# Expert weights applied to summed second products, with ScalarE's squares and roundings and the router's steps in another order

## What is computed

```python
# attention layer, feed-forward
u, g = split(y @ w_swiglu.T); x = x + u * silu(g) @ w_out.T
# experts, on z = layernorm(x)
probs = softmax(z @ w_router.T); top = argmax(probs); weight = probs[top]
h = z @ w_fc[e].T                          # e = 0, 1
a = square(where(h >= 0, h, 0.5 * h))
x = x + sum over e of (top == e) * weight * (a @ w_proj[e].T)
```

## Time and profile before

| | us |
|---|---|
| median of 3 runs | 862.57 (862.54 to 862.64) |
| the profiled execution | 862.95 |
| its span, first to last instruction | 860.8 |
| busy: TensorE, VectorE, ScalarE, GpSimd | 851.4, 683.3, 554.7, 370.6 |
| granted TensorE clock | 1.00 over the span |

### The profile page before, as it was taken

How to read it: one execution, slowest core, us unless ns; L and a number is a source line. 1 busy time by engine, 2 the same in 40 slices (tenths; PEclk the granted TensorE clock), 3 DMA queues, 4 the chain that set the end, 5 groups by cost and what they waited for, 6 DMA issues and landing times.

```text
span 860.8 us, 14422 instructions
## 1 busy us (share of the span) xinstructions
PE 851.4 (99%) x4618; PEld 731.0 (85%) x4618; DVE 683.3 (79%) x1075; ACT 554.7 (64%) x1009; POOL 370.6 (43%) x215
## 2 busy tenths in 40 slices
PE   8999999999999999999999999999999999999998
PEld 7888888888888888888888888888888889878767
DVE  5777777777777777777777777888888878779897
ACT  5666666666666666666666666666777656676563
POOL 2555454544555554445445555544454433220000
DMA  7212214010101010010101010101101000679740
GB/s 271 98 51 76 73 52 167 24 49 24 49 24 49 24 49 25 30 43 24 49 24 49 24 49 24 48 25 28 46 24 49 26 1 11 239 282 410 308 147 13
DMA packets 19529, 66.25 MB, mean 77 GB/s; under 512 B 2224, under 2 KB 2992, under 8 KB 19120
## 3 DMA queue, kind: packets, MB, share of 16 engines
q1 hardware_dynamic: 19072, 64.88, 20.9%
q10 hardware_dynamic: 432, 1.05, 0.3%
HBM read 65.66 MB, written 0.26 MB: 77 GB/s over the span
## 4 chain that ended last, share of the span: by engine, by line
PE 91%; issue 4%; DVE 2%; DMA 1%; POOL 1%; ACT 0%; POOLq 0%; ACTq 0%; SPq 0%; DVEq 0%
PE kv_ps L879 11%; PE f_ps L866 11%; PE v_bank L784 10%; PE v_bank L785 10%; PE v_bank L786 10%; PE k_bank L784 10%; PE k_bank L785 10%; PE k_bank L786 10%; PE kv_ps L1178 2%; PE kv_ps L1160 1%; DMA early<-in_wk 1%; PE f_ps L949 0%; PE f_ps L1050 0%; PE v_bank L968 0%; DMA ctx_raw<-in_ctx 0%
## 5 line engine op out<-in xcount | busy, mean ns | idle before, releaser
L461 POOL TENSOR_TENSOR ksum_acc<-ksum_acc,kf 128x1024 f32<-128x1024 f32 x97 | 233.0, 2402 | 86.7 <-DVE kf L1284 86.7
L454 POOL TENSOR_TENSOR ctx_lo<-ctx_raw,ctx_hi 128x512 fp32r<-128x512 f32 x92 | 119.7, 1301 | 274.0 <-ACT ctx_hi L532 274.0
L540 ACT ACTIVATE keys<-k_bank,bias_cols 64x512 fp32r<-64x512 f32 (+1 forms) x194 | 131.5, 678 | 148.6 <-PE k_bank L786 146.2
L1260 DVE SCALAR_TENSOR_TENSOR keys<-k_bank,bias_cols,keys 64x512 fp32r<-64x512 f32 (+1 forms) x194 | 143.2, 738 | 83.7 <-ACT keys L540 80.4
L1277 DVE TENSOR_TENSOR kf<-f_ps,fb 128x256 f32<-128x256 f32 x392 | 148.6, 420 | 16.8 <-ACT fb L557 5.6
L784 PE MATMUL v_bank<-wv_hi,ctx_lo 128*128 128x512 f32 x388 | 152.3, 392 | 0.0
L785 PE MATMUL v_bank<-wv_lo,ctx_hi 128*128 128x512 f32 x388 | 152.1, 392 | 0.0
L784 PE MATMUL k_bank<-ctx_hi,wk_lo 128*128 128x512 f32 (+1 forms) x392 | 151.4, 386 | 0.0
L785 PE MATMUL k_bank<-ctx_lo,wk_hi 128*128 128x512 f32 (+1 forms) x392 | 151.1, 385 | 0.0
L786 PE MATMUL v_bank<-wv_hi,ctx_hi 128*128 128x512 f32 x388 | 151.0, 389 | 0.0
L786 PE MATMUL k_bank<-ctx_hi,wk_hi 128*128 128x512 f32 (+1 forms) x392 | 149.9, 383 | 0.0
(11 more groups left out here) (245 smaller groups left out, 979.0 us busy)
## 6 DMA issues: line engine op xcount, KB each, us to landing
ctx_raw<-in_ctx SPq DMA_DIRECT2D x46, 512.0 KB, 3.3
early<-in_stream SPq DMA_DIRECT2D x15, 1024.0 KB, 8.4
raw<-in_stream SPq DMA_DIRECT2D x12, 1024.0 KB, 8.7
early<-in_stream SPq DMA_DIRECT2D x8, 512.0 KB, 4.2
early<-in_ctx SPq DMA_DIRECT2D x2, 512.0 KB, 6.1
early<-in_wv SPq DMA_DIRECT2D x1, 1024.0 KB, 7.8
early<-in_wq SPq DMA_DIRECT2D x1, 1024.0 KB, 9.2
early<-in_wo SPq DMA_DIRECT2D x1, 1024.0 KB, 7.1
```

Source lines behind the costliest of these rows:

```text
L454: pool.tensor_tensor(ctx_lo[:, s, :, cols], raw[:, :, t % 2 * P:(t % 2 + 1) * P], ctx_hi[:, s, :, cols].bitcast(f32), ALU.subtract).then_i ...
L461: pool.tensor_tensor(ksum_acc[:, :].rearrange("p (j f) -> p j f", f=P), ksum_acc[:, :].rearrange("p (j f) -> p j f", f=P), kf[:, t % 2, :, ...
L540: act.activation(keys_2[rows, s, 2 * m + h, 0:n], src[rows, 0:n], ACT.Identity, bias=bias_cols[rows, KC + m:KC + m + 1]).then_inc(k_hi_rea ...
L1260: dve.scalar_tensor_tensor(out=keys_2[other, s, 2 * m + h, 0:n], in0=src[rows, 0:n], scalar=bias_cols[rows, KC + m:KC + m + 1], in1=keys_2 ...
```

## The change

- The router's weight is no longer part of `hid`. `hid` is the plain square, and is made by ACT (`expert_square`, from DVE's maximum in `gate`) in place of DVE. The second products of each expert are summed apart, expert 0 in `wide_ps[0]`, expert 1 in `wide_ps[1]` and the two last halves, and DVE adds each sum times its weight to `x1`: a further `wide_added(GP[3], ...)` in block 6.
- One second product is fp32 and seven are in three passes (before: two and six). So 52 half groups are rounded, not 50.
- ACT's roundings in the experts stand elsewhere: none in block 0, GP[1] in block 1, then two groups in each of blocks 2 to 5, and one in 6 and 7. DVE's pieces are set to match.
- The router: the logits are scaled on DVE behind the maximum of block 0, the exponentials stand on ACT behind its square, and the six steps behind the pieces of block 3. A dummy exponential ahead of the experts sets ACT's table. POOL subtracts the mean that DVE subtracted at the output.
- SwiGLU: Silu on ACT in place of Sigmoid on ACT and a product on DVE; a dummy Silu ahead of it.
- Attention: denominators and numerators in another order on PE; two of ACT's roundings are split around other steps, its copy of the router weights stands behind the exponentials; DVE runs one piece ahead of the wait for `rms_ready` and two behind it (before: two, then one).

```diff
-         GF_[5], GP[3], GF_[6], GP[4], GF_[7], *GP[5:8]]
-FIRST = 2
+SPLIT = [..., *GF_[0:4], GP[1],
+         GF_[4], GP[2], GF_[5], GP[3], GF_[6], GP[4], GF_[7], *GP[5:8]]
-        wide_ps = kv_bank[0]
+        wide_ps = [kv_bank[0], kv_bank[2]]
...
             rstd(3, 8, 1)
+            pool.wait_ge(actT_done, 8)
+            pool.tensor_scalar(x1[:, :], x1[:, :], stat[:, 18:19], None, ALU.subtract).then_inc(mean_back, 1)
...
             turned_high(3)
+            act.activation(stat[:, 30:31], half[:, :], ACT.Silu)
             weight_high(GD[0])
...
-                act.activation(gate[:, n % 2, :], k_ps[n % 2], ACT.Sigmoid).then_inc(gateg_ready, 1)
+                act.activation(gate[:, n % 2, :], k_ps[n % 2], ACT.Silu).then_inc(gateg_ready, 1)
...
             turned_high(4)
+            act.activation(stat[:, 30:31], half[:, :], ACT.Exp)
             def expert_high(n):
                 act.wait_ge(group_used, GF_[n] + 1)
-                if n >= 2:
-                    act.wait_ge(hid_ready, nd + n - 1)
                 act.activation(gate[:, n % 2, :], k_ps[n % 2], ACT.Copy, scale=0.5)\
                    .then_inc(fc_half_ready, 1)
-            act.wait_ge(logit_neg_ready, 1)
-            act.activation(logit[:, 3:5], logit[:, 0:2], ACT.Exp, bias=logit[:, 2:3]).then_inc(expl_ready, 1)
+            def expert_square(n):
+                if n >= 2:
+                    act.wait_ge(hidT_done, nd + n - 1)
+                act.wait_ge(fc_ready, n + 1)
+                act.activation(hid[:, n % 2, :], gate[:, n % 2, :], ACT.Square).then_inc(hid_ready, 1)
             for n in range(2 * nd):
                 expert_high(n)
                 if n:
                     hidden_turned(nd + n - 1)
-                for g in (GF_[4:5], GP[2:3], GF_[5:6], (GP[3], GF_[6]), (GP[4], GF_[7]), GP[5:7], GP[7:8], ())[n]:
+                expert_square(n)
+                if n == 0:
+                    act.wait_ge(logit_neg_ready, 1)
+                    act.activation(logit[:, 3:5], logit[:, 0:2], ACT.Exp, bias=logit[:, 2:3]).then_inc(expl_ready, 1)
+                for g in ((), GP[1:2], (GF_[4], GP[2]), (GF_[5], GP[3]), (GF_[6], GP[4]), (GF_[7], GP[5]), GP[6:7], GP[7:8])[n]:
                     weight_high(g)
...
-            denominators(range(3))
+            denominators(range(4)).then_inc(den_done, 1)
...
-            denominators(range(3, 4)).then_inc(den_done, 1)
-            denominators(range(4, NPAIR)).then_inc(den_done, 1)
+            denominators(range(4, 6))
             numerators(0)
+            denominators(range(6, NPAIR)).then_inc(den_done, 1)
             numerators(1)
...
-            low_pieces(1, 3)
+            low_pieces(1, 2)
+            dve.wait_ge(rms_ready, 1)
+            low_pieces(2, 4)
             dve.wait_ge(wr_hi_ready, 1)
...
-            low_pieces(26, 27)
+            low_pieces(26, 28)
...
             for n in range(2 * nd):
                 dve.wait_ge(fc_half_ready, n + 1)
                 h = gate[:, n % 2, :]
-                link(dve.tensor_tensor(h, k_ps[n % 2], h, ALU.max))
-                dve.scalar_tensor_tensor(out=hid[:, n % 2, :], in0=h, scalar=logit[:, 6 + e:7 + e], in1=h,
-                                         op0=ALU.mult, op1=ALU.mult).then_inc(hid_ready, 1)
-                if n > FIRST:
+                dve.tensor_tensor(h, k_ps[n % 2], h, ALU.max).then_inc(fc_ready, 1)
+                if n == 0:
+                    router_logits()
+                if n > 1:
                     hidden_low(nd + n - 1)
-                low_pieces(*((27, 28), (28, 30), (30, 34), (34, 38), (38, 42), (42, 44), (44, 48), (48, 50))[n])
+                low_pieces(*((28, 29), (29, 32), (32, 36), (36, 40), (40, 44), (44, 48), (48, 50), (50, 52))[n])
+                if n == 3:
+                    router_weights()
+                if n == 6:
+                    dve.wait_ge(mean_back, 1)
+                    wide_added(GP[3], logit[:, 6:7])
```

More of the change, by code:

```diff
@@ L1147, in hidden_turn, with down_outs, hidden_down @@
                 transposes(f_ps[n % 2], hid[:, n % 2, :]).then_inc(hidT_done, 1)
[L1149 to L1155, removed]
+            def down_outs(g, last_one):
+                return [(half_ps[b][:, 0:D // 2], halves[b]) for b in range(2)] if last_one else [(wide_ps[g > GP[3]], full)]
+            def hidden_down(n, g):
                 wait_loaded(pe, g)
                 pe.wait_ge(hidT_ready, n + 1)
[L1158 to L1163, removed]
+                for k in range(KC):
+                    last = pe.matmul(wide_ps[0], hid_T2[n % 2][:, k, :], raw(g)[:, k, :], start=k == 0, stop=False)
                 last.then_inc(group_used, 1)
@@ L1544, in _ @@
                 dve.wait_ge(group_used, GU[n] + 1)
-                dve.tensor_tensor(hid[:, n % 2, :], v_ps[n % 2], e, ALU.mult).then_inc(hid_ready, 1)
+                dve.tensor_tensor(hid[:, n % 2, :], v_ps[n % 2], gate[:, n % 2, :], ALU.mult).then_inc(hid_ready, 1)
                 if n:
@@ L1574, in _, with router_logits @@
[L1574 to L1575 removed]
+            low_pieces(26, 28)
+            def router_logits():
+                dve.wait_ge(logit_done, 1)
+                dve.wait_ge(rstd_ready, 3)
+                dve.tensor_tensor(stat[:, 13:14], stat[:, 8:9], stat[:, 8:9], ALU.mult)
+                link(dve.tensor_scalar(logit[:, 0:2], v_ps[0][:, 0:2], stat[:, 8:9], None, ALU.mult))
+                link(dve.scalar_tensor_tensor(out=logit[:, 0:2], in0=v_ps[0][:, 2:4], scalar=stat[:, 8:9], in1=logit[:, 0:2],
+                                              op0=ALU.mult, op1=ALU.add))
+                link(dve.tensor_reduce(logit[:, 2:3], logit[:, 0:2], AX.X, ALU.max))
+                dve.tensor_scalar(logit[:, 2:3], logit[:, 2:3], -1.0, None, ALU.mult).then_inc(logit_neg_ready, 1)
@@ L1594, in _ @@
                     dve.wait_ge(group_used, GP[-1] + 1)
-                dve.scalar_tensor_tensor(out=hid[:, 0, cols], in0=half_ps[b][:, 0:D // 2], scalar=stat[:, 18:19],
-                                         in1=x1[:, cols], op0=ALU.subtract, op1=ALU.add).then_inc(out_ready, 1)
+                dve.scalar_tensor_tensor(out=hid[:, 0, cols], in0=half_ps[b][:, 0:D // 2], scalar=logit[:, 7:8],
+                                         in1=x1[:, cols], op0=ALU.mult, op1=ALU.add).then_inc(out_ready, 1)
 def kernel(**inputs):
```

75 lines of the change are left out of this document (36 added, 39 removed).

## The result

| us | before | after |
|---|---|---|
| median of 8 runs | 862.62 (862.51 to 863.05) | 865.89 (864.25 to 866.26) |
| the profiled execution, its span | 862.95, 860.8 | 866.26, 864.2 |
| granted TensorE clock, mean of the span | 1.00 | 0.998 |

The medians differ by 3.3 us, and the change makes the kernel slower. The ratio estimated over all executions is 1.0033, with an interval of 1.0024 to 1.0041 (the medians alone give 1.0038). The forecast was 864.1 us, within 0.2% of no change. The median lies 1.8 us above it and 0.3 above the upper end of the range; by the ratio (1.0033 of 862.57 is 865.4) the result is just inside the range. The case that came true is "slower by over 0.2%", which had 0.36. Six of the eight executions show a mean clock of 0.998 and take 865.82 to 866.26; the two at 1.000 take 864.25 and 864.92.

What follows compares the result with a forecast made beforehand. TensorE, with 91% of the chain of waits, was taken to bound the kernel. Experts -1.34 - 0.64 + 3.83, rounded to +1.8, and attention -0.3 gave +1.5 us on 862.57: 864.1 us, range 862.2 to 865.6.

Steps and rivals of the forecast that it cites:

- slower by over 0.2%: Outcome case for the whole kernel: measured time over 0.2% above before; takes the second, third and fourth rival, chance 0.36.
- the loop: Experts: DVE max, ACT square, first w_hi, four w_lo pieces, next max strictly in turn; 6.88 us against PE's 6.04.
- Everything from there to the end is the same work.: After the last turn of hid, turn(7) at 853.83: nothing further changes, so its +1.8 us carries to the end.
- The loop and no early gain: Rival: same loop with square and handovers at upper bounds (+0.4), or attention's 0.3 lost; 864.5 to 865, chance 0.28.
- attention's end: Denominator j=3 ahead of the transposes and an earlier GpSimd root: about 0.4 and more, of which 0.3 us reaches the end.
- The stalls: Experts: PE waits of 0.84, 0.87 and 2.12 us before turns 5, 6 and 7 of hid; turn 4 just in time.
- the two late pieces: Attention's end: two DVE pieces behind rms_ready take 2.27 us, freeing DVE for the reciprocal at 763.3, not 763.60.
- the removed stall at 762.29: Attention's end: PE's stall of 0.45 us should go, but PE's wait at 768.53 grows.
- The removed work: Experts: first turn no longer waits for the softmax, -1.34 us; second fp32 product in three passes, -0.64; Silu and GpSimd's subtraction, nothing.
- The rival of throughput: Rival, experts: summed engine work fits under PE's turn, so order does not bind and PE never waits; 860.3, chance 0.12.
- GpSimd holding DVE: Rival, experts: the 2.10 us mean subtraction blocks DVE's pieces, starting the loop up to 2 us later; 866, chance 0.05.
- an uncovered Silu: Rival, SwiGLU: Silu is not cheap or cover fails, the table load's 1.4 us show in PE; 865.5, chance 0.03.

Runs made afterwards that it cites:

- the experiment: Kernel before with only attention's new order of denominators and numerators on PE and ACT's two roundings split: 862.15 us against 862.83, ratio 0.9993.
- the first experiment: Changed kernel with one of the block's two groups rounded on ACT ahead of its square in blocks 2 to 5: 860.12 us, ratio 0.9966.
- The softmax experiment: Changed kernel with the six router steps of block 3 ahead of that block's four DVE pieces, not behind them: 863.46 us, ratio 1.0006.

## Why the prediction was right and wrong

**The step that failed** is the sentence behind the loop: "Everything from there to the end is the same work." The work was the same, its clock was not. A wait of 2.12 us was forecast (2.04 came), and the prediction did not ask how fast PE runs behind a wait that long. 10 of 14 executions of the changed kernel have the lower mean clock. The one of them with a profile shows the fall behind this wait, where it costs 1.56 us; the medians of the two groups differ by 1.2 (866.0 against 864.8). That carried the median out of the range. No rival had it; the trace of before has no wait above 1.17 us in this stage.

The clock is not all of the miss. At full clock 864.8 is 0.25% above 862.62, so even without the fall the forecast of "within 0.2%" fails, though narrowly: 864.1 had left 0.2 us to that line. The price is that of the rival *The loop and no early gain* (864.5 to 865). Of its two conditions the first came about, a turn 0.05 us longer (it had 0.06); the second did not, since attention's end gained more than was forecast.

**The loop** held. Forecast 6.88 us a turn, measured 6.93: the hand-over from max to square was 0.09, not 0.04; square to `w_hi` 0.53 for 0.51; `w_hi` to `w_lo` 1.08 for 1.10. Over group 3 it was 8.23 (8.17). Block 6 to 7 was 5.45 for 5.33. From 817.77 on, the maxima took 0.35 more than forecast over the whole stage, and the last `hid` another 0.07. The turn of group 4 was forecast as just in time and came 0.24 late.

**The stalls.** Idle of 0.84, 0.87 and 2.12 was forecast and 0.69, 0.72 and 2.04 is shown, though the turns did lose 0.93, 0.94 and 2.2 us. The forecast had counted from start to start. A shown idle leaves out what an instruction otherwise overlaps with the one in front (840.65 is the end of the pass before 841.34; unstalled, the turn would have started at 840.48) and the slower first transposes (0.66 for 0.60): about 0.23 a wait.

**Attention's end** was undersized: 0.3 forecast, 0.6 measured (745.04 to 768.04 here, 744.94 to 768.53 before; 0.62 in the experiment). PE's, DVE's and GpSimd's timelines after the change, as in the earlier trace rows:

```profile
745.04 1.10 PE L1087 MATMUL v_bank<-ksum_k,qf_T 128*128 128x64 f32 x8
...
750.02 0.40 PE L1012 MATMUL kv_ps<-ident,att 128*128 128x128 f32 x2
...
768.04 0.44 PE L1012 MATMUL kv_ps<-ident,att 128*128 128x128 f32 x2 [0.54 <-DVE att L1523]
```

```profile
760.79 2.36 DVE L351 TENSOR_TENSOR w_lo<-raw,w_hi 128x1024 fp32r<-128x1024 f32 x2 [1.39 <-POOL stat L511]
...
763.14 1.75 DVE L1528 RECIPROCAL kv_parts<-kv_parts 128x256 f32<-128x256 f32 x1
```

```profile
758.35 1.62 POOL L448 TENSOR_TENSOR stat<-stat,half 128x2 f32<-128x2 f32 x1 [2.47 <-DVE rms_eps L1504]
...
760.21 0.54 POOL L511 TENSOR_TENSOR stat<-stat,half 128x1 f32<-128x1 f32 x1
```

0.57 of it is there by 750.02: the 0.24 of two denominators, the stall of 0.18, and again the overlap that a stall hides. None of it is lost later, so it was wrong to let only 0.3 of 0.4 through because of the two late pieces: the reciprocal moved with the rest, by 0.46 (763.60 to 763.14) and by 0.56 if counted from the first denominators, and the stall of about 1.1 that was to grow there is 0.54, with one of 0.19 ahead of it. What was right is that the removed stall at 762.29 gives nothing.

**The removed work** came as costed: the first turn at 812.33 against a forecast of 812.84 - 0.3, the second fp32 product 6.00 for 6.68 (822.17 to 828.17), Silu nothing, GpSimd's subtraction nothing.

**The sum** at full clock: +1.5 was forecast, and +1.9 came by the spans of the two profiled executions (860.8 and 862.7), +2.2 by the medians (862.62 and 864.8). The profiled times, forecast 864.5 and measured 864.72, agree better than that by luck: the execution before stood 0.33 above its median, and this one did not. Two errors nearly cancel at the last turn: the maximum of group 2 came 0.2 earlier than forecast (817.77 for 818.29 - 0.3), and the loop took 0.4 longer, so the turn stands 0.20 later (853.73 for 853.83 - 0.3). About 0.2 more came behind it, 0.07 of that by 857.01; the rest is not located. The rival of throughput fell (its price, 860.3, is what the first experiment gives once the loop is open: 860.12); so did GpSimd holding DVE, and an uncovered Silu.

**What stays open:** why one execution falls to half clock and the next does not, with the same starts to 0.01 us. The softmax experiment kept it in eight of ten behind a wait of 2.05. Kernels without a wait above 1.2 us in this stage have executions at 0.998 as well, 1.2 to 1.7 us slower than their others: the kernel before in 4 of 27, 0 of 27, 3 of 18 and 1 of 10 (by batch), Silu alone in 1 of 10, the `rms_ready` order alone in 2 of 10. No profile here shows where those fell. Taken together, kernels with a last wait of about 2 us fell in 18 of 39 executions, the kernel before in 8 of 82 of these batches: the wait makes the fall more frequent, and it is not the only way to it.

## What to carry to other kernels

Before giving a full engine's work to a less full one, write down the turn of hand-overs between the two as their lists are ordered: if each waits for the other within one turn, the turn is the sum of both sides, whatever the busy shares say. The cure is an order in which each has something that depends on nothing standing ahead of what it must wait for (here one rounded group ahead of the square: 4.7 us with no instruction changed). And cost a new wait of TensorE twice: its length, and the clock behind it.

## What the runs showed of the hardware

- Behind a wait of 2.04 us PE's granted clock was 0.67 and then 0.50 in the two stretches of 2 us that followed, and 0.98 in the next. 10 of 14 executions of that kernel have the lower mean clock; behind its waits of 0.69 and 0.72 the profile shows no fall. With two matmuls in the gap none of ten fell, on another chip.
- GpSimd's root took 1.62 us beside a piece of DVE's (L448, at 758.35) and 0.54 alone (L511, at 760.21). The first writes two columns and the second one, but that is not the reason: at 807.98 L448 writes one column beside DVE's pieces and takes 1.46. The pieces beside them took their usual time (two in 2.35 at 807.82), and so did four in 4.62 from 770.95, while GpSimd's subtraction L516 ran from 770.10 to 772.19. In these rows it was never DVE that was slowed.
- A 512-column square from SBUF took 0.63 us on ACT, a 512-column copy from PSUM 0.57 to 0.60.
- A table load for Silu took 1.28 us, as the exponential's.
